# A two-sublayer attention block on one Trainium2 core: scores issued together, and DMAs that were cut in four issued whole

## The reference

```python
x = x + 0.5 * ffn(layernorm(x))     # 16 heads of 64, 8 experts, top 2 of 8 picked twice
x = x + attn(layernorm(x))          # linear attention: a product of two states per head
x = x + 0.5 * ffn(layernorm(x))
```

## Time and profile before

| | |
|---|---|
| time, median of 3 runs | 2452.96 us (2450.31 to 2454.0) |
| the profiled execution | 2450.31 us, span 2448.5 us |
| TensorE, mean granted clock | 0.996 |
| busy: TensorE, ScalarE, VectorE, GpSimd | 95%, 85%, 78%, 47% |
| DMA engines, mean busy share | 54.2% for SyncE's queue |

### The profile page before, as it was taken

One profiled execution on the slowest core, in us unless ns is written; L12 is line 12 of the kernel. 1 busy time (PEld: TensorE's weight loads), 2 busy tenths in 40 slices (PEclk: granted clock), 3 DMA queues, 4 the chain that ended last, 5 costly groups with the idle time before them and its releaser, 6 DMA issues.

```text
span 2448.5 us, 120555 instructions
## 1 busy us (share of the span) xinstructions
PE 2328.4 (95%) x49920; PEld 2151.2 (88%) x49920; DVE 1919.5 (78%) x3498; ACT 2072.4 (85%) x6373; POOL 1162.5 (47%) x1126
## 2 busy tenths in 40 slices
PE   3999999999999999999999999999999999999997
PEld 3889999899989898898988888988899998889897
DVE  4887877878878778878878787788887888887774
ACT  3988888888888888888888888888888988888885
POOL 3354645545535545445455355454454454454431
PEclk9999999999999999999999999999999999999998
DMA  4555555555555655555555555555555555555553
GB/s 123 161 157 153 153 157 152 168 162 162 168 157 161 172 154 164 163 156 159 167 163 158 157 157 173 153 164 167 151 165 162 163 166 160 160 154 163 163 168 103
DMA packets 660701, 388.23 MB, mean 159 GB/s; under 512 B 232512, under 2 KB 585664, under 8 KB 660160
## 3 DMA queue, kind: packets, MB, share of 16 engines
q1 hardware_dynamic: 659728, 379.67, 54.2%
q10 hardware_dynamic: 432, 0.85, 0.1%
HBM read 191.64 MB, written 188.74 MB: 155 GB/s over the span
## 4 chain that ended last, share of the span: by engine, by line
PE 77%; DVE 10%; ACT 7%; issue 5%; POOL 1%; DMA 0%; SPq 0%; ACTq 0%; DVEq 0%; POOLq 0%
PE psT L466 17%; PE psS L421 14%; PE psT L483 6%; PE psS L509 6%; PE psT L434 6%; PE psT L509 5%; PE psT L485 5%; PE psT L484 5%; ACT PB L783 5%; PE psT L478 5%; PE psT L448 3%; DVE NMAX L661 2%; DVE QK L722 2%; DVE ST L745 1%; DVE NMAX L677 1%
## 5 line engine op out<-in xcount | busy, mean ns | idle before, releaser
L783 ACT ACTIVATE PB<-psS,NMAX 128x256 f32<-128x256 f32 x2048 | 944.6, 485 | 147.5 <-DVE NMAX L661 84.2
L466 PE MATMUL psT<-V,PT 128*64 128x64 f32 x16384 | 545.1, 224 | 17.6 <-issue 15.6
L466 PEld LDWEIGHTS psT<-V,PT 128*64 128x64 f32 x16384 | 505.1, 138 | 56.6 <-issue 22.3
L722 DVE TENSOR_TENSOR QK<-psT,QK 128x512 fp32r<-128x512 f32 x512 | 335.4, 686 | 222.5 <-ACT QK L792 221.3
L421 PE MATMUL psS<-QK 64*128 64x256 f32 x6144 | 489.1, 293 | 0.0
L783 ACT ACTIVATION_READ_ACCUMULATOR PB<-psS,NMAX 128x1 f32 x2048 | 445.1, 217 | 0.0
L661 DVE TENSOR_REDUCE NMAX<-psS 128x2 f32<-128x512 f32 x512 | 329.2, 684 | 120.7 <-PE psS L421 120.2
L421 PEld LDWEIGHTS psS<-QK 64*128 64x128 f32 x6144 | 402.9, 187 | 14.1 <-issue 4.7
L891 POOL TENSOR_TENSOR BT<-MT,diagv 128x1024 f32<-128x1024 f32 x128 | 306.8, 2397 | 142.1 <-DMA MT<-MIXd 141.9
L792 ACT ACTIVATE QK<-psT 128x512 fp32r<-128x512 f32 x512 | 294.7, 623 | 39.5 <-PE psT L485 32.0
L677 DVE TENSOR_REDUCE NMAX<-psS 128x4 f32<-128x1024 f32 x256 | 311.9, 1219 | 17.5 <-PE psS L421 11.0
(11 more groups left out here) (119 smaller groups left out, 4560.3 us busy)
## 6 DMA issues: line engine op xcount, KB each, us to landing
Vd<-VM SPq DMA_DIRECT2D x512, 128.0 KB, 2.3
V<-Vd SPq DMA_DIRECT2D x512, 128.0 KB, 3.1
AOd<-AO SPq DMA_DIRECT2D x256, 256.0 KB, 2.6
AR<-AOd SPq DMA_DIRECT2D x256, 256.0 KB, 4.2
PJd<-PJ SPq DMA_DIRECT2D x64, 512.0 KB, 3.1
PR<-PJd SPq DMA_DIRECT2D x256, 128.0 KB, 2.8
MIXd<-MIX SPq DMA_DIRECT2D x64, 128.0 KB, 2.2
MT<-MIXd SPq DMA_DIRECT2D x64, 128.0 KB, 2.9
```

The lines of the kernel that those rows point to most:

```text
L466: last = eng.matmul(M[64 * u:64 * u + 64, (t * NT + it) * DH:(t * NT + it + 1) * DH], PT[:, t, jt, cols], V[:, pm % 2, 4 * r + t, jt, :], ...
L722: eng.tensor_tensor(QK[:, 1, ab], bank("qk", m).rearrange("p (k t) -> p k t", k=2), QK[:, 0, ab].bitcast(F32), ALU.subtract).then_inc(free ...
L783: eng.activation(PB[:, ab, j, it, :], psS[:, ab, j, it, :], ACT.Exp, bias=NMAX[:, ab, j, it:it + 1], accum_out=SUM[:, p % 2, it, 4 * r + t ...
```

## The change

Two things are changed. Order: on TensorE `scores(n, 1)` follows `scores(n, 0)` at once, ahead of `values` and `output`. On VectorE the maximum L677 follows L661 at once, and what stood between them (in r = 1 the statistics of a row and the update with `output`, in r = 2 `largest`, in r = 3 `highest`) comes after it; some of the blocks behind it change places. ScalarE's and GpSimd's lists are as they were. DMAs: `PARTS` is gone. Four transfers (Vd store, V load, PR load, AR load) are issued whole instead of in four pieces, and the waits on them count 16 instead of 64.

```diff
             def store_values(q, half):
-                for i in range(PARTS):
-                    own = slice(8 // PARTS * i, 8 // PARTS * (i + 1))
-                    eng.dma_start(stored[:, own, :], mixed[:, own, :]).then_inc(s_vw[half], 16)
+                eng.dma_start(Vd[q % 2].rearrange("(k q x) -> q k x", q=P, x=NT * DH)[:, 8 * half:8 * half + 8, :],
+                              VM[:, half].rearrange("p g a x -> p (g a) x")).then_inc(s_vw[half], 16)
...
             def load_values(q, half):
-                for i in range(PARTS):
-                    own = slice(H * NT * DH // PARTS * i, H * NT * DH // PARTS * (i + 1))
-                    eng.dma_start(loaded[:, own], stored[:, own]).then_inc(s_value[q % 2], 16)
+                eng.dma_start(V[rows, q % 2].rearrange("p h n d -> p (h n d)"),
+                              Vd[q % 2].rearrange("(p x) -> p x", p=P)[rows]).then_inc(s_value[q % 2], 16)
...
-                    for i in range(PARTS):
-                        own = slice(16 // PARTS * i, 16 // PARTS * (i + 1))
-                        eng.dma_start(AR[:, own, :], stored[:, own, :]).then_inc(s_ar, 16)
+                    eng.dma_start(AR[:, :, :], AOd[q % 2].rearrange("(g q x) -> q g x", q=P, x=NT * DH)).then_inc(s_ar, 16)
...
                 if works(n):
                     scores(n, 0)
+                    scores(n, 1)
                 if r == 2 and runs(p + 1):
                     values(p + 1, 0)
                 if r == 3 and runs(p + 1):
                     values(p + 1, 1)
                 if r == 1 and runs(p - 2):
                     output(p - 2)
-                if works(n):
-                    scores(n, 1)
                 if works(n - 1):
                     product(n - 1)
...
                     for j in range(2):
                         eng.tensor_reduce(NMAX[:, 0, j, :], psS[:, 0, j, :, :], AX_X, ALU.max, negate=True).then_inc(s_max)
-                if r == 1 and runs(p + 3):
-                    wait_x(eng, p + 3)
-                    statistics(s_stat, 4 * (p + 3), 0, x_of(p + 3))
-                if r == 1 and runs(p - 2):
-                    for it in range(NT):
-                        xs = x_of(p - 2)[:, it, :]
-                        wait_full(eng, "output", p - 2, it)
-                        eng.scalar_tensor_tensor(xs, bank("output", p - 2, it)[:, 0:C], 0.5, xs, ALU.mult, ALU.add).then_inc(freed("output", p - 2, it))
-                if r == 2 and runs(q):
-                    eng.wait_ge(s_pick, at + 6)
-                    largest(1, GM[:, :, :])
-                if r == 3 and runs(q):
-                    highest(at + 9)
-                if works(n):
                     eng.wait_ge(s_score, 2 * n + 2)
                     eng.tensor_reduce(NMAX[:, 1, :, :], psS[:, 1, :, :, :], AX_X, ALU.max, negate=True).then_inc(s_max)
```

More of the change, by code:

```diff
@@ L20 @@
 SHARES = 4
-PARTS = 4
 MASKS = 4
@@ L317, in load_values @@
                 eng.wait_ge(s_split, 4)
-                eng.wait_ge(s_vw[half], 16 * PARTS * (q + 1))
+                eng.wait_ge(s_vw[half], 16 * (q + 1))
                 wait_full(eng, "product", 4 * (q - 2) + 3)
-                loaded = V[rows, q % 2].rearrange("p h n d -> p (h n d)")
-                stored = Vd[q % 2].rearrange("(p x) -> p x", p=P)[rows]
-                for i in range(PARTS):
-                    own = slice(H * NT * DH // PARTS * i, H * NT * DH // PARTS * (i + 1))
-                    eng.dma_start(loaded[:, own], stored[:, own]).then_inc(s_value[q % 2], 16)
+                eng.dma_start(V[rows, q % 2].rearrange("p h n d -> p (h n d)"),
+                              Vd[q % 2].rearrange("(p x) -> p x", p=P)[rows]).then_inc(s_value[q % 2], 16)
             for n in QUARTERS:
@@ L370, in sync_program @@
                         wait_full(eng, "values", q - 1, 1, a)
-                    stored = PJd[q % 2].rearrange("(g r x) -> r g x", r=P, x=NT * DH)
-                    for i in range(PARTS):
-                        own = slice(8 // PARTS * i, 8 // PARTS * (i + 1))
-                        eng.dma_start(PR[:, own, :], stored[:, own, :]).then_inc(s_pr, 16)
+                    eng.dma_start(PR[:, :, :], PJd[q % 2].rearrange("(g r x) -> r g x", r=P, x=NT * DH)).then_inc(s_pr, 16)
                 if r == 3 and runs(p + 1):
@@ L428, in values @@
                 eng.wait_ge(s_bt[half], q + 1)
-                eng.wait_ge(s_pr, 16 * PARTS * (q + 1))
+                eng.wait_ge(s_pr, 16 * (q + 1))
                 for k in range(8):
@@ L455, in product @@
                 if r == 0:
-                    eng.wait_ge(s_value[pm % 2], 32 * PARTS * (pm // 2 + 1))
+                    eng.wait_ge(s_value[pm % 2], 32 * (pm // 2 + 1))
                 M = bank("product", m)
@@ L472, in expand @@
                 if b == 0:
-                    eng.wait_ge(s_ar, 16 * PARTS * (q + 1))
+                    eng.wait_ge(s_ar, 16 * (q + 1))
                 eng.wait_ge(s_mb[b], q + 1)
@@ L682, in vector_program @@
                     eng.reciprocal(RSUM[:, :], SUM[:, (p - 1) % 2].rearrange("p n h -> p (n h)")).then_inc(s_rsum)
+                if r == 1 and runs(p - 2):
+                    for it in range(NT):
+                        xs = x_of(p - 2)[:, it, :]
+                        wait_full(eng, "output", p - 2, it)
+                        eng.scalar_tensor_tensor(xs, bank("output", p - 2, it)[:, 0:C], 0.5, xs, ALU.mult, ALU.add).then_inc(freed("output", p - 2, it))
                 if r == 2 and attends(p - 3):
@@ L685, in vector_program @@
                     statistics(s_bstat, 4 * nth[p - 3], 2, AA)
+                if r == 1 and runs(p + 3):
+                    wait_x(eng, p + 3)
+                    statistics(s_stat, 4 * (p + 3), 0, x_of(p + 3))
                 if r == 1 and runs(q):
@@ L690, in vector_program @@
                     first(F1[:, :, :], at + 4)
+                if r == 2 and runs(q):
+                    eng.wait_ge(s_pick, at + 6)
+                    largest(1, GM[:, :, :])
                 if r == 3 and runs(q):
+                    highest(at + 9)
                     first(F2[:, :, :], at + 10)
@@ L795, in copy_values @@
                 if q >= 1:
-                    eng.wait_ge(s_vw[half], 16 * PARTS * q)
+                    eng.wait_ge(s_vw[half], 16 * q)
                 for a in range(2):
```

8 lines of the change are left out of this document (2 added, 6 removed).

## The result

The changed kernel is slower: 2475.14 us (median; 2473.61 to 2477.27) against 2451.64 us (2449.28 to 2454.0) for the kernel before on the same chip, a ratio of 1.0116 with a 95% interval of 1.0090 to 1.0143. The profiled execution has a span of 2468.7 us at a granted clock of 0.995 (before: 2448.5 us at 0.996), so the clock is not the cause.

What follows compares the result with a forecast made beforehand. TensorE was taken as the bound nearly everywhere, except ScalarE in some quarters and BT-held VectorE in r = 1 of A passes. Terms -22 (r = 1), +2 (lost luck), +6 (TensorE), -3 (ends) made -17: 2433 us, range 2420 to 2450.

Steps and rivals of the forecast that it cites:

- What bounds the kernel: TensorE nearly everywhere, ScalarE in r = 0 and A passes' r = 3, VectorE held by BT in A passes' r = 1.
- VectorE is freed wholly: Rival, r = 1 of A passes: 22 quarters reach TensorE's 9.2 us, -32 us there, 2421 us in all; chance 0.10.
- VectorE order in r = 1: A passes: ScalarE's wait for L677 goes and L722 moves to L700's end, gaining 0.49 us in a hit pass.
- X + 7.27: Forecast length in us of r = 1 in A passes, X being L661's start after the scores; before, X + 7.76.
- Earlier BT: r = 1 of A passes: MT issued 1.1 us earlier, so BT starts earlier and X falls 0.5 us in 22 passes.
- the queue being as full as now or emptier: r = 1 of A passes: assumption behind BT starting at 1217.0 to 1217.6 in place of 1218.68 in pass 31.
- case (a): r = 1 of A passes: BT starts after L622, L742 is held to BT's end, and X = 2.0 us.
- BT gives nothing: Rival, r = 1 of A passes: only L722's 0.49 us is gained, -6 us in all, 2444 us; chance 0.14.
- TensorE order: r = 2 and r = 3: fewer switches but a wait for ScalarE's copies, 38 x 0.15 = +6 us.
- The other merged loads have microseconds to spare in the middle: Middle of the kernel: merged loads other than V of r = 0 have time to spare; no cost in the sum.
- Ends: Kernel's start and end: fewer issues save up to 1.8 us at either end, taken as -3 us for both.
- Slower: Rival: second scores wait behind ScalarE's copies, net about 0.2 us in 192 quarters, +13 us, 2463 us; chance 0.12.

Runs made afterwards that it cites:

- e3: The changed kernel with the V loads alone back in four pieces: 2454.96 us, 1.0020 of the kernel before.
- e4: The kernel before with the new order and the V loads alone whole, other transfers in four pieces: 2482.59 us, ratio 1.0130.
- e2: The kernel before with the new order alone, all four transfers still in four pieces: 2458.59 us, ratio 1.0030.
- e9: The kernel before, with GpSimd's BT in r = 1 waiting until VectorE is through L626: 2415.9 us, ratio 0.9866.
- e6: The kernel before with the new order on TensorE and VectorE in r = 1 alone: 2442.08 us, ratio 0.9956.
- e1: The kernel before with all four transfers issued whole, its order as it was: 2483.78 us, ratio 1.0134.
- e16: The changed kernel with the first-half V load, still whole, issued in r = 3 behind the product's AOd store: 2439.0 us, 0.9960 of the kernel before.
- e5: The changed kernel with each V load in four issues of 16 rows, packets of 8192 B: 2482.1 us, 1.0123 of the kernel before.
- e13: The changed kernel with gaps in V's SBUF rows, so one issue moves packets of 2048 B: 2488.08 us, 1.0153 of the kernel before.
- e15: The kernel before with BT waiting for VectorE's L626 and the V loads alone whole: 2448.41 us, ratio 0.9993.
- e17: The kernel before with BT waiting for L626, V loads whole, the first half issued behind the product's store: 2408.65 us, ratio 0.9841.
- e18: The kernel before with BT waiting for L626, V loads in four pieces, the first half issued behind the product's store: 2410.7 us, ratio 0.9846.

## Why the prediction was wrong

It gave 2433 us with a range to 2450 and 0.76 for faster. The time was 2475 us. The profiled spans differ by +20 us where the sum had -17. Of these 37 us the whole V load makes 19 to 23 (after against e3, e4 against e2, passes 10 to 59), the new order in r = 2 and r = 3 some 10, r = 1 5 and the ends 3. By its own steps:

- **What bounds the kernel**: right. The 22 held quarters were priced at 32 us in "VectorE is freed wholly", and e9, which frees them, gained 33 us.
- **VectorE order in r = 1**: right. ScalarE's wait for L677 went, L722 (now L706) follows the copy directly. X + 7.27 was forecast; the held passes show X + 7.19 in e6 and X + 7.17 in the kernel after. The other 7 of its 25 A passes have L647 at about 1.0 us and take 9.43 us. The forecast had 9.2 us for TensorE's own work there: in the new order the product starts 0.26 us later in r = 1 of A passes (3.65 us against 3.39).
- **Earlier BT, 22 x 0.5 = 11 us**: wrong in size. MT went out 1.71 us after MIXd in pass 31 (forecast 1.8) and on the mean 1.1 us earlier than before (2.37 us after MIXd against 3.48), but its landing took 4.4 us in place of 2.9. The step "the queue being as full as now or emptier" was wrong: MT now follows 512 KB of V that are still in flight. BT started after L608 (L622 before), as in case (a), but at 1234.88 and so not early enough: L647 stayed at 2.6 to 3.0 us in held passes. The mean of X fell by 0.3 us, mostly through three more passes in which BT happened to start late. L608 keeps its 682 ns in every run, so nothing here tells whether it would be held. The rival "BT gives nothing" had this right. In all, r = 1 gave 15 us where the terms 22 x (0.49 + 0.5) less the lost luck gave 20.
- **TensorE order, +6 us**: right in the path that it named, wrong in what the order costs. In r = 3 the second scores come at 0.96 us and the product at 2.95 us, as forecast (0.95 and 3.0), and against before the product starts only 0.06 us later. But by e2 r = 2 and r = 3 lose 16.5 us, and halts make up all of it (17.8 us). In the kernel after r = 2 lost 0.19 us in A passes, all in halts, and 0.18 us in B, of which 0.06 is the later product and most of the rest lies in `expand` behind it.
- **"The other merged loads have microseconds to spare in the middle"**: this step failed, and with it the one on halts. It asked when the data is needed, and never what the transfer does to others on the same 16 DMA engines. The halts of TensorE were seen beforehand and put at "some us either way" without a cause, and so at nothing in the sum. They grew by 30.6 us, 25 of them in r = 3, and in A passes ScalarE did not cover for them there, as the forecast had it for small costs (10.04 us in place of 9.38). And they have a cause: the packet with TensorE's next instructions comes too late. The V load, whole and right ahead of the product of r = 3, delays it (2.51 us in place of 1.64, and 1.26 us long in place of 1.02). e4 and e1 show that it is the V load, and e16 that the same load 6 us later is harmless. e5 and e13 show that neither long packets nor the single issue is the whole reason. The new order adds to the halts by itself (e2), without a cause that a run isolates.
- **Ends, -3 us**: not separated by any run. The profiled spans differ by 20.2 us and the middle by 21.3, so at most a microsecond or so was gained there.

No rival foresaw it. "Slower" had the right sign by another mechanism, a wait behind ScalarE's copies, which cost 0.06 us or less in r = 2 and r = 3. Its time of 2463 us would not have been met either. Where halts had been seen and had no cause, 0.12 for slower was too little.

The Trainium skill, "DMA: Bandwidth & Descriptors", section "Rules for kernel authors", advises to coalesce many small transfers into a large one, and names 64 KB as the size under which overhead prevails. The pieces here, 128 KB, are above that, so the case does not contradict it. For 128 KB made into 512 KB no run shows a gain: 1.3% lost in place (e15 against e9), nothing won when moved (e17 against e18).

Open: why the new order alone brings halts and its parts don't add up, why four issues help only together with short packets, and when TensorE asks for a packet. What was seen is only when the packet runs and that TensorE resumes 1.2 to 1.6 us after its end.

## What to carry to other kernels

A transfer that has time to spare can still cost. Ask what else must cross the DMA engines while it fills them: instructions for a busy engine, and small loads issued behind it. "Issue" idle that grows inside one group of matmuls is a reason to look at the DMA view for q8 packets, and to move the bulk load behind that group before cutting or merging it; halts that recur at the same place of every 256 instructions point there too. And where two engines exclude each other, a wait on the one with time to spare may be worth more (1.3% in e9) than a new order on the other (0.4% in e6).

## What the runs showed of the hardware

- TensorE's instruction packets share the DMA engines with data: 0.96 us for one in the kernel before, 1.4 us for the same one behind the V load in pass 31, and a start 3.3 us after the scores in place of 0.5. There is one packet for 256 of TensorE's records (400 for 102401).
- A halt ends 1.2 to 1.8 us after such a packet ends and lies at record 193 or 194 modulo 256: 690 halts of over 0.3 us inside products, in the traces of all twenty kernels, without an exception.
- Four issues are not in themselves gentler than one: pieces by rows with packets of 8192 B, 1.6 us from the first to the last start (e5, 58.5 us of issue idle), halt TensorE as much as one issue with packets of 2048 B (e13, 58.3). Pieces by columns with packets of 2048 B, 2.0 us from first to last (e3, 26.4), halt it less.
- A load of 128 KB issued 1.28 us behind one of 512 KB lands in 4.4 us, behind four of 128 KB in 2.9 us. Over the runs it is 4.2 to 4.8 us with V in one issue or by rows and 2.7 to 3.0 us with V in pieces by columns; e17, with V whole and 3.2 us, is the exception.
- A VectorE instruction of 0.29 us with two SBUF operands lasts 2.36 us under a GpSimd product (1235.21 to 1237.57, the product ending at 1237.42); with GpSimd held back it takes 291 ns on the mean (e9).
